# Flamingo block, one core: rows gathered per tile with an inverted slot table, and shared groups split four and three

## Chip, cores and metric

One core of one Trainium2 chip runs the whole program in one launch. The time is device microseconds from the first to the last instruction, with what lies around them; the median of 3 runs stands for the kernel.

## What is computed

Input `x` is 32 sequences of 112 rows of 256 numbers, 3584 rows in all. First comes gated cross attention to a context of 375 rows (16 heads), then a mixture of experts: every row passes through two shared experts and through the two of 14 routed experts that its gate likes best.

```python
x = x + tanh(g_xattn) * xattn(layernorm(x), ctx, Wq, Wk, Wv, Wo, bo)
xf = layernorm(x).reshape(3584, 256)
gates = softmax(xf @ router_w)                 # 14 experts
top_v, top_i = top_k(gates, 2)                 # weights, divided by their sum
routed = sum over the row's two experts of weight * ffn_e(xf)
shared = ffn_s0(xf) + ffn_s1(xf)
x = x + tanh(g_ffn) * (routed + shared)
# ffn(h) = silu((rmsnorm(h) * rms_w) @ W1) @ W2, W1 256x512, W2 512x256
```

## The kernel before

Every product is made of float32r parts: a value is split into a high part (ScalarE's cast) and a low one (VectorE's subtraction), and three matmuls hi*hi, hi*lo, lo*hi are summed.

**Attention** (`attend`, 0 to about 1125 us) goes over 16 pairs of sequences in a loop. SP issues its loads in program order: `x_in` for pair p+2, keys, residual rows, and beside them one routed expert per pair, whose weights POOL scales and splits for `w_split` in HBM. It stores the rows after attention in `x2_rows`, and the normalised rows with one more number in `h_rows` (257 a row). Besides, it prepares the buffer `sorted` in HBM, 69 tiles of 128 rows of 258 numbers: at the start it is filled with zeros from `fill` (L366), and after pair 0 the column D of all its rows is set to the numbers of spare rows, from `spare` (L389), 4 bytes at a time.

**Front** (`front`) transposes all rows, computes the gate, and works on items, one for each group of 512 rows and shared expert: `hidden(i)` is 24 matmuls of 512 columns into four banks, ScalarE's silu and cast, VectorE's subtraction (`split_hidden`), then `output(i)`, 48 matmuls of 256 columns, which VectorE adds to `acc` (`accumulate`). `BEFORE` = 5 groups, 10 items, come here. PE's order is hidden(i), output(i-1). Between its own duties VectorE makes the plan: for each row and choice k the slot (place in the sorted order, in which each expert has whole tiles), and for each of the 69 tiles its expert. When the slots are known, POOL writes to `sorted`: for 14 half groups SP loads the rows to SBUF twice (`load_rows`, 28 loads in four buffers), POOL adds number of destination and weight (L997), and issues 4 indirect DMAs of 128 rows each (L1002), 56 in all.

**Routed stage** (`routed_experts`) goes over 69 tiles. A tile's rows come as one plain load from `sorted`, six buffers ahead, issued by ACT; POOL copies each row's number and weight (`take_meta`); PE transposes the rows, 6 matmuls of 512 columns make the hidden part, 4 transposes, 8 output matmuls; ScalarE and VectorE scale both halves by the weight (L1504, L1538); POOL scatters the 128 result rows to `y_rows` (L1417). Weights of experts stand in a ring of five places; the places also hold the front's buffers, so expert e is loaded only when those are done. `w_ready` is counted in order of the experts.

**Tail** (`shared_after`): the other 2 groups, 4 items. SP loads `y_rows` back (two blocks a group), POOL adds both to `acc` (L1596, 14 additions of 128x1024), VectorE accumulates the shared parts, SP stores the groups.

Of the kernel before, what the change touches and what calls it, by code (L numbers as in the profile page):

```python
# [16 lines left out]
ALU = mybir.AluOpType  # L17
# [34 lines left out]
def fuse_weights(nc, io, sb, banks, ctx):  # L52

    if True:
# [13 lines left out]
        bias_in, bias_ok, fill_ok = sem("bias_in"), sem("bias_ok"), sem("fill_ok")  # L68
        sb["zeroed"], sb["fill_ok"] = zeroed, fill_ok
# [12 lines left out]
        def gpsimd(pool):  # L82
# [5 lines left out]
            nc.gpsimd.memset(sb["fill"][:], 0.0).then_inc(zeroed, 1)  # L88
            nc.gpsimd.iota(sb["spare"][:], pattern=[[P, SLOT_TILES]], base=TOPK * TOK, channel_multiplier=1
                           ).then_inc(fill_ok, 1)  # L90
            pool.wait_ge(zeroed, 2)
            pool.wait_ge(fill_ok, 1)
# [95 lines left out]
def attend(nc, io, sb, banks):  # L188

    with ExitStack() as ctx:  # L190
# [41 lines left out]
        x_landed, slots_filled = sem("x_landed"), sem("slots_filled")  # L232
# [77 lines left out]
        def _(sp):  # L310
# [52 lines left out]
            sp.wait_ge(sb["zeroed"], 2)  # L363
            sp.wait_ge(sb["fill_ok"], 1)
            empty = sb["fill"][:].unsqueeze(1).to_broadcast([P, SLOT_TILES, ROW])
            sp.dma_start(io["sorted"].rearrange("(t p) d -> p t d", p=P), empty).then_inc(slots_filled, 16)  # L366
            load_x(1)

            def body(p, jobs):
# [13 lines left out]
                if not first and not last:  # L383
# [3 lines left out]
            sp.wait_ge(slots_filled, 16)  # L387
# [9 lines left out]
            sp.wait_ge(slots_filled, 32)  # L397
# [302 lines left out]
        def _(dve):  # L700
# [124 lines left out]
            for s in (4, 3, 2, 1):  # L825
# [11 lines left out]
               ("spare", [P, (TOK * TOPK + E * (P - 1)) // P], I32), ("kvT_hi", [P, 2, MW], F32R), ("kvT_lo", [P, 2, MW], F32R),  # L837
# [6 lines left out]
ROW = D + 2  # L844
WSIZE = 2 * HID + 4 * D
RING = 5
BEFORE = 5
COUNT_AFTER = 1
PRODUCTS = [("hi", "hi"), ("lo", "hi"), ("hi", "lo")]
# [28 lines left out]
def front(nc, io, sb, banks, ctx):  # L878

    if True:  # L880
# [21 lines left out]
        meta = buf("meta", [P, TILES, TOPK, 2])  # L902
# [6 lines left out]
        slot_f = buf("slot_f", [P, TILES, TOPK])  # L909
        slot = buf("slot", [P, TILES, TOPK], U32)  # L910
# [5 lines left out]
        acc, rows = sb["acc"], sb["rows"]  # L916

        RB = 4
# [7 lines left out]
        consts, step, counted, meta_ok, slot_ok = sem("consts"), sem("step"), sem("counted"), sem("meta_ok"), sem("slot_ok")  # L926
        acc_landed = [sem(f"acc_landed{i}") for i in range(2)]
        rows_landed = [sem(f"rows_landed{b}") for b in range(RB)]
        rows_sent = [sem(f"rows_sent{b}") for b in range(RB)]
        meta_set = sem("meta_set")  # L930
        h_done, silu_done, hid_hi_ok, hid_lo_ok = sem("h_done"), sem("silu_done"), sem("hid_hi"), sem("hid_lo")
        o_done, acc_done = sem("o_done"), sem("acc_done")
        H_BANK, O_BANK, COUNT_BANK = banks[0:4], banks[4:6], banks[6:8]
# [4 lines left out]
        def sync(sp):  # L938
# [9 lines left out]
            def load_rows(u):  # L948
                two = by_group(io["h_rows"], u // 2)[:, 2 * (u % 2):2 * (u % 2) + 2, 0:D]
                for k in range(TOPK):  # L950
                    sp.dma_start(rows[:, u % RB, :, k, 0:D], two).then_inc(rows_landed[u % RB], 16)

# [8 lines left out]
            for g in range(BEFORE):  # L961
# [4 lines left out]
            for g in range(BEFORE, GROUPS):  # L966
                sp.dma_start(acc[:, 4 * g:4 * g + 4, :], by_group(io["x2_rows"], g)).then_inc(acc_landed[1], 16)
            sp.wait_ge(step, PLAN_END)
            load_experts(sp, io, sb, [0])
            for u in range(RB, 2 * GROUPS):  # L970
                sp.wait_ge(rows_sent[u % RB], 64 * (u // RB))
                load_rows(u)
            for e in (1, 2):
                sp.wait_ge(h_done, 16 * e)
                load_experts(sp, io, sb, [e])

        def gpsimd(pool):
# [11 lines left out]
            for k in range(TOPK):  # L989
                nc.gpsimd.iota(meta[:, :, k, 0].bitcast(I32), pattern=[[4 * P, GROUPS], [1, 4]], base=k * TOK,  # L990
                               channel_multiplier=4).then_inc(meta_ok, 1)
            pool.wait_ge(meta_ok, 2 + TOPK)
            pool.wait_ge(slot_ok, 1)
            for u in range(2 * GROUPS):
                b = u % RB
                pool.wait_ge(rows_landed[b], 32 * (u // RB) + 32)
                nc.gpsimd.tensor_copy(rows[:, b, :, :, D:ROW], meta[:, 2 * u:2 * u + 2, :, :]).then_inc(meta_set, 1)  # L997
                pool.wait_ge(meta_set, u + 1)
                for t in range(2):
                    for k in range(TOPK):  # L1000
                        at = slot[:, 2 * u + t, k:k + 1]
                        nc.gpsimd.indirect_dma_start(io["sorted"], bass.IndirectOffsetOnAxis(ap=at, axis=0),  # L1002
                                                     rows[:, b, t, k, :], None).then_inc(rows_sent[b], 16)

        def tensor(pe):
# [65 lines left out]
            for i in range(len(items)):  # L1071
                hidden(i)
                if i > 0:
                    output(i - 1)
# [37 lines left out]
        def vector(dve):  # L1112
# [667 lines left out]
```

## Time and profile before

| | |
|---|---|
| median of 3 runs (lowest, highest) | 1613.81 us (1612.7, 1614.38) |
| profiled execution | 1619.13 us, its span 1617.4 us |
| mean granted TensorE clock | 0.968 |
| busy in the span | PE 1509.5 us (93%), VectorE 1126.5 (70%), ScalarE 1018.3 (63%), POOL 459.8 (28%) |
| DMA | 160.89 MB, 99 GB/s on average |

A group of instructions is named by line, engine, operation and tile; "idle before" is the time in which its engine waited just before it, with what released it. "issue" means that the profile shows nothing that the engine waited for. The granted clock is a share of full speed, 0.50 being 1.2 GHz and 1.00 being 2.4 GHz. In the table by stretch the columns are PE, weight loads (PEld), VectorE (DVE), ScalarE (ACT) and POOL, then granted clock, busy share of the DMA engines and GB/s.

### The profile page before, as it was taken

What the parts mean: (1) busy time and instruction counts of PE and PEld (TensorE: products, weight loads), DVE (VectorE), ACT (ScalarE), POOL (GpSimd) and SP (SyncE); (2) the same over time, 40 slices, a digit from 0 to 9 for tenths busy, and PEclk for the clock granted to TensorE, in tenths of its full rate; (3) what the DMA queues carried; (4) which work ended last, traced back from release to release, by engine and by line L of the source; (5) the groups of instructions that cost most, each with busy time, mean ns of one, the idle gap of its engine ahead of it and who ended that gap; (6) DMA issues with size and microseconds to landing.
All of it is one profiled execution on the core that took longest, in us unless ns stands there. A gap on an engine that the chain in (4) does not pass through costs nothing. (4 is left out here: it accounts for less than half of the span.)

```text
span 1617.4 us, 34486 instructions
## 1 busy us (share of the span) xinstructions
PE 1509.5 (93%) x10102; PEld 1398.8 (86%) x10102; DVE 1126.5 (70%) x2788; ACT 1018.3 (63%) x2641; POOL 459.8 (28%) x742
## 2 busy tenths in 40 slices
PE   6797999999999999999999999996896689999997
PEld 6697999999999999999999999996684578888887
DVE  5686888788888888888888888884861234444446
ACT  4575777777777777777777777774531235555552
POOL 1003134131241322413314033111047203333338
PEclk9898999999999999999999999998897699999999
DMA  9315302112021121211211202101637435664234
GB/s 266 78 16 40 103 13 97 74 50 97 17 101 66 50 97 39 79 72 44 97 74 44 87 29 97 68 15 52 247 100 215 164 119 180 235 229 134 80 125 192
DMA packets 89921, 160.89 MB, mean 99 GB/s; under 512 B 20688, under 2 KB 73184, under 8 KB 86272
## 3 DMA queue, kind: packets, MB, share of 16 engines
q1 hardware_dynamic: 74784, 135.29, 26.3%
q0 software_dynamic: 6000, 16.45, 2.8%
q10 hardware_dynamic: 9072, 8.33, 1.8%
q8 instruction: 36, 0.59, 0.2%
q14 instruction: 29, 0.24, 0.0%
HBM read 94.06 MB, written 65.98 MB: 99 GB/s over the span
## 5 line engine op out<-in xcount | busy, mean ns | idle before, releaser
L631 ACT ACTIVATE prob<-bank,nmax 112x375 f32<-112x375 f32 x512 | 296.2, 579 | 247.2 <-DVE nmax L720 245.8
L703 DVE TENSOR_TENSOR pT_lo<-bank,pT_hi 125x336 fp32r<-125x336 f32 x512 | 257.0, 502 | 101.8 <-ACT pT_hi L643 99.2
L720 DVE TENSOR_REDUCE nmax<-bank 112x1 f32<-112x375 f32 x512 | 276.4, 540 | 33.7 <-PE bank L499 27.7
L553 PE MATMUL bank<-keep_ident,prob 112*125 112x112 f32 x1536 | 254.4, 274 | 31.1 <-DVE pT_lo L703 30.9
L553 PEld LDWEIGHTS bank<-keep_ident,prob 112*125 112x125 f32 x1536 | 227.0, 189 | 60.3 <-issue 46.2
L643 ACT CAST pT_hi<-bank 125x336 fp32r<-125x336 f32 x512 | 223.4, 436 | 1.3 <-PE bank L553 1.2
L497 PE MATMUL bank<-attend_wvo_hi,zT_hi 128*112 128x256 f32 x512 | 179.2, 350 | 0.6 <-DVE zT_lo L703 0.6
L497 PE MATMUL bank<-attend_kvT_hi,qp_hi 128*112 128x376 f32 x512 | 171.7, 335 | 0.8 <-ACT prob L631 0.7
L498 PE MATMUL bank<-attend_kvT_hi,qp_lo 128*112 128x376 f32 x512 | 171.4, 335 | 0.0
L499 PE MATMUL bank<-attend_kvT_lo,qp_hi 128*112 128x376 f32 x512 | 171.4, 335 | 0.0
L636 ACT ACTIVATE prob<-prob,prob_inv 112x375 f32<-112x375 f32 x256 | 153.4, 599 | 1.6 <-DVE prob_inv L726 0.4
L497 PE MATMUL bank<-xnT_hi,attend_wqk_hi 128*128 128x224 f32 x512 | 141.8, 277 | 3.9 <-DVE xnT_lo L703 3.9
L498 PE MATMUL bank<-attend_wvo_hi,zT_lo 128*112 128x256 f32 x512 | 144.4, 282 | 0.0
L499 PE MATMUL bank<-attend_wvo_lo,zT_hi 128*112 128x256 f32 x512 | 143.8, 281 | 0.0
L497 PE MATMUL bank<-pT_hi,kv_hi 125*128 125x448 f32 x384 | 141.9, 370 | 1.5 <-DVE zT_lo L703 1.5
L499 PE MATMUL bank<-xnT_lo,attend_wqk_hi 128*128 128x224 f32 x512 | 142.7, 279 | 0.0
L498 PE MATMUL bank<-xnT_hi,attend_wqk_lo 128*128 128x224 f32 x512 | 141.8, 277 | 0.0
L499 PE MATMUL bank<-pT_lo,kv_hi 125*128 125x448 f32 x384 | 140.5, 366 | 0.0
L498 PE MATMUL bank<-pT_hi,kv_lo 125*128 125x448 f32 x384 | 140.2, 365 | 0.0
L442 POOL TENSOR_SCALAR rs<-mv 112x1 f32<-112x1 f32 x32 | 7.0, 219 | 439.3 <-DVE mv L774 439.2
L729 DVE TENSOR_SCALAR prob<-prob,prob_inv 112x375 f32<-112x375 f32 x256 | 118.6, 463 | 9.1
L1417 POOL DMA_INDIRECT y_rows<-over_y,keep_tile_meta x69 | 66.7, 967 | 190.7 <-DVE over_y L1538 187.7
(226 smaller groups left out, 3809.1 us busy)
## 6 DMA issues: line engine op xcount, KB each, us to landing
w_split<-we_split SPq DMA_DIRECT2D x14, 2048.0 KB, 6.9
keep_weights<-w_split SPq DMA_DIRECT2D x14, 2048.0 KB
we_in<-in_w SPq DMA_DIRECT2D x28, 512.0 KB, 5.9
sorted<-keep_fill SPq DMA_DIRECT2D x1, 8901.0 KB, 35.3
keep_tile_in<-sorted ACTq DMA_DIRECT2D x63, 129.0 KB
keep_rows<-h_rows SPq DMA_DIRECT2D x28, 256.0 KB
over_y_all<-y_rows SPq DMA_DIRECT2D x14, 512.0 KB, 8.9
kv_in<-in_ctx SPq DMA_DIRECT2D x32, 187.5 KB
```

The lines of the kernel that those rows point to most:

```text
L442: nc.gpsimd.tensor_scalar(rs2[:, 0, 0:1], mv2[:, 1:2], LN_EPS, None, ALU.add).then_inc(ln2_pool, 1)
L497: nc.tensor.matmul(out, a[0], b_[0], start=start, stop=False)
L498: nc.tensor.matmul(out, a[1], b_[0], start=False, stop=False)
L499: return nc.tensor.matmul(out, a[0], b_[1], start=False, stop=stop)
L553: last = nc.tensor.transpose(T[s % 2][0:MP, c * N:(c + 1) * N], prob[:, s % NB, c * MP:(c + 1) * MP], ident[0:N, 0:N])
L631: nc.scalar.activation(prob[:, s % NB, :], S[s % 3][0:N, 0:M], ACT.Exp, bias=nmax[:, s % NB:s % NB + 1], accum_out=psum_[:, s % NB:s % NB ...
L636: nc.scalar.mul(prob[:, s % NB, :], prob[:, s % NB, :], pinv[:, s % NB:s % NB + 1]).then_inc(norm_act, 1)
L643: nc.scalar.copy(dst, T[s % 2][0:MP, 0:MC * N].rearrange("p (c n) -> p c n", c=MC)).then_inc(pT_hi, 1)
L703: return nc.vector.tensor_tensor(dst, src, hi.bitcast(F32), ALU.subtract)
L720: nc.vector.tensor_reduce(nmax[:, s % NB:s % NB + 1], S[s % 3][0:N, 0:M], AX, ALU.max, negate=True).then_inc(max_ready, 1)
L729: nc.vector.tensor_scalar(prob[:, s % NB, :], prob[:, s % NB, :], pinv[:, s % NB:s % NB + 1], None, ALU.mult).then_inc(norm_dve, 1)
L1417: nc.gpsimd.indirect_dma_start(io["y_rows"], bass.IndirectOffsetOnAxis(ap=at, axis=0), y[:, t % YB, :], None).then_inc(y_sent[t % YB], 16)
```

## The change

`sorted`, its fill, the spare numbers, the 28 loads and the 56 scatters are gone. Instead the plan is inverted on the chip: for each of the 7168 pairs of row and choice the slot is divided into tile number and lane (place in the tile). 56 columns of 128 pairs are taken in 14 chunks of 4. For a chunk VectorE (`make_hot`) compares with counting numbers, which gives a one-hot matrix of lanes (128x128 a column) and one of tiles, the latter times two numbers that name the row; PE multiplies them (`place_rows`, 4 matmuls of 138 columns a chunk) and sums all in one bank. `decode` makes `from_row` and `to_row` of it, for each of the 69 tiles 128 numbers. POOL then gathers a tile's rows from `h_rows` with an indirect DMA (`fetch`), six ahead, and then one behind every scatter. The weights are no longer applied in the tile but in the tail, where VectorE adds `y_all` times weight (56 operations of 128x256) in POOL's place. Four shared groups are ahead of the routed tiles (8 items) and three behind them (6 items). The buffers lie elsewhere: expert 1's place is free after h_done 16 as before, expert 2's when decode is done.

```diff
@@ attend: sync @@
-            sp.wait_ge(sb["zeroed"], 2)
-            sp.wait_ge(sb["fill_ok"], 1)
-            empty = sb["fill"][:].unsqueeze(1).to_broadcast([P, SLOT_TILES, ROW])
-            sp.dma_start(io["sorted"].rearrange("(t p) d -> p t d", p=P), empty).then_inc(slots_filled, 16)
             load_x(1)
...
-            spare_rows = io["sorted"].rearrange("(t p) d -> p t d", p=P)[:, :, D:D + 1]
-            sp.dma_start(spare_rows, sb["spare"][:].bitcast(F32).unsqueeze(2), allow_slow_non_contiguous=True
-                         ).then_inc(slots_filled, 16)
@@ sizes @@
-BEFORE = 5
+BEFORE = 4
+COLS = TOPK * TILES
+CHUNK = 4
+CHUNKS = COLS // CHUNK
+CHUNKS_IN = {3: (0, 1, 2), 4: (3, 4, 5, 6), 5: (7, 8, 9, 10), 6: (11, 12, 13)}
@@ front: sync @@
-            sp.wait_ge(w_lo, 6)
-            for u in range(RB):
-                load_rows(u)
...
             sp.wait_ge(step, PLAN_END)
+            sp.wait_ge(nums_ok, 4)
+            sp.wait_ge(lanes, 4)
             load_experts(sp, io, sb, [0])
-            for u in range(RB, 2 * GROUPS):
-                sp.wait_ge(rows_sent[u % RB], 64 * (u // RB))
-                load_rows(u)
-            for e in (1, 2):
-                sp.wait_ge(h_done, 16 * e)
-                load_experts(sp, io, sb, [e])
+            sp.wait_ge(h_done, 16)
+            load_experts(sp, io, sb, [1])
+            sp.wait_ge(rows_of_ok, 2)
+            load_experts(sp, io, sb, [2])
@@ front: tensor @@
+            def place_rows(c):
+                pe.wait_ge(hot_ok, 3 * c + 3)
+                for m in range(CHUNK):
+                    last = nc.tensor.matmul(PLACE_BANK[:, 0:2 * SLOT_TILES], lane_hot[:, c % 2, m, :],
+                                            tile_hot[:, c % 2, m, :, :].rearrange("p n t -> p (n t)"),
...
+                last.then_inc(hot_used, 1)
             for i in range(len(items)):
                 hidden(i)
+                for c in CHUNKS_IN.get(i - 1, ()):
+                    place_rows(c)
                 if i > 0:
                     output(i - 1)
...
+            output(len(items) - 1)
             sb["turn_first_rows"](pe)
-            output(len(items) - 1)
@@ front: vector @@
+            def make_hot(c):
...
+                if c >= 2:
+                    dve.wait_ge(hot_used, c - 1)
...
+                nc.vector.tensor_tensor(placed[:], up_to(SLOT_TILES), each(tile_no, SLOT_TILES), ALU.is_equal).then_inc(tile_eq, 1)
+                nc.vector.tensor_tensor(lane_hot[:, b, :, :], up_to(P), each(lane_no, P), ALU.is_equal).then_inc(hot_ok, 1)
+                dve.wait_ge(tile_eq, c + 1)
+                for n in range(2):
+                    nc.vector.tensor_tensor(tile_hot[:, b, :, n, :], placed[:], each(place[n], SLOT_TILES), ALU.mult
+                                            ).then_inc(hot_ok, 1)
             plan_owner()
+            for c in CHUNKS_IN[3]:
+                make_hot(c)
             for i in range(4, len(items)):
                 for j in range(4):
                     split_hidden(i, j)
+                if i - 1 == max(CHUNKS_IN):
+                    decode()
                 for t in range(4):
                     accumulate(i - 1, t)
+                for c in CHUNKS_IN.get(i, ()):
+                    make_hot(c)
@@ routed_experts: gpsimd @@
+            def fetch(t):
+                if t >= HB:
+                    pool.wait_ge(h_turned, t - HB + 1)
+                at = sb["from_row"][:, t:t + 1]
+                nc.gpsimd.indirect_dma_start(h_in[:, t % HB, :], None, io["h_rows"], bass.IndirectOffsetOnAxis(ap=at, axis=0)
+                                             ).then_inc(h_landed[t % HB], 16)
+            pool.wait_ge(sb["sem_rows_of_ok"], 2)
+            for t in range(HB):
+                fetch(t)
@@ shared_after @@
+        Y_IN = {1: order[0:2], 2: order[2:4], 3: order[4:6], 4: order[6:7]}
-                    nc.gpsimd.tensor_tensor(whole, whole, y_all[:, k, 4 * g:4 * g + 4, :], ALU.add).then_inc(y_added, 1)
+            def add_routed(g):
+                dve.wait_ge(y_landed[g], 32)
+                for k in range(TOPK):
+                    for t in range(4 * g, 4 * g + 4):
...
+                        nc.vector.scalar_tensor_tensor(out=acc[:, t, :], in0=y_all[:, k, t, :],
+                                                       scalar=sb["weight_of"][:, k, t:t + 1], in1=acc[:, t, :],
+                                                       op0=ALU.mult, op1=ALU.add).then_inc(y_added, 1)
```

VectorE in the front, after the plan: before (a row is a run of like instructions; L1302 is `split_hidden`, L1297 `accumulate`):

```order
L1270 CAST keep_ring_of<-over_owner 1x69
L1302 TENSOR_TENSOR keep_hid_lo<-keep_silu,over_hid_hi 128x512 x4
L1297 TENSOR_TENSOR keep_acc<-bank,keep_acc 128x256 x4
L1302 TENSOR_TENSOR keep_hid_lo<-keep_silu,over_hid_hi 128x512 x4
L1297 TENSOR_TENSOR keep_acc<-bank,keep_acc 128x256 x4
```

and now, where each chunk is four rows and the first three chunks stand ahead of item 4's splits (L1340):

```order
L1308 CAST keep_ring_of<-over_owner 1x69
L1257 TENSOR_TENSOR over_placed<-over_count_up,over_tile_no 128x276
L1258 TENSOR_TENSOR over_lane_hot<-over_count_up,over_lane_no 128x512
L1261 TENSOR_TENSOR over_tile_hot<-over_placed,over_place_4920 128x4x69
L1261 TENSOR_TENSOR over_tile_hot<-over_placed,over_place_4921 128x4x69
...
L1340 TENSOR_TENSOR keep_hid_lo<-keep_silu,over_hid_hi 128x512 x4
L1335 TENSOR_TENSOR keep_acc<-bank,keep_acc 128x256 x4
L1257 TENSOR_TENSOR over_placed<-over_count_up,over_tile_no 128x276
```

The run of splits that came right behind the plan now comes behind three chunks, and between the splits of items 4, 5, 6 and 7 stand four, four and three chunks.

POOL, from the front into the routed stage, before:

```order
L997 COPY keep_rows<-front_meta 128x4x2
L1002 DMA sorted<-keep_rows,front_slot 8832x258 x4
L1408 COPY keep_tile_meta<-keep_tile_in 128x2 x3
L1417 DMA y_rows<-over_y,keep_tile_meta 16000x256
L1408 COPY keep_tile_meta<-keep_tile_in 128x2
```

and now:

```order
L979 CAST over_pad_row<-over_pad_i 128x69
L1446 DMA keep_tile_in<-h_rows,keep_from_row 128x257 x6
L1455 DMA y_rows<-over_y,keep_to_row 16000x256
L1446 DMA keep_tile_in<-h_rows,keep_from_row 128x257
L1455 DMA y_rows<-over_y,keep_to_row 16000x256
```

The copies went, and a gather follows each scatter; the 56 scatters in the front have nothing in their place.

VectorE in the tail now (before, L1639 and L1646 stood there alone; L1676 is `add_routed`):

```order
L1685 TENSOR_TENSOR keep_hid_lo<-keep_silu,over_hid_hi 128x512 x8
L1676 SCALAR_TENSOR_TENSOR keep_acc<-over_y_all,keep_weight_of,keep_acc 128x256 x16
L1668 TENSOR_TENSOR keep_acc<-bank,keep_acc 128x256 x4
L1685 TENSOR_TENSOR keep_hid_lo<-keep_silu,over_hid_hi 128x512 x4
L1676 SCALAR_TENSOR_TENSOR keep_acc<-over_y_all,keep_weight_of,keep_acc 128x256 x16
```

Two groups' additions stand behind the splits of items 1, 2 and 3 each, and one group's behind those of item 4.

## Rows read from the trace of the kernel before

**Rows 1.** Page, part 2: PE busy, in tenths, in 40 slices of 40.4 us
```profile
PE   6797999999999999999999999996896689999997
```

**Rows 2.** Busy time by stretch: start:end, length; then each engine's us (x instructions)
```profile
50.00:60.00 10.00, 5.43 (x23) 5.44 (x24) 5.13 (x16) 4.10 (x13) 0.26 (x2) 0.50 0.12 42
1153.00:1211.00 58.00, 54.39 (x313) 47.86 (x314) 43.96 (x99) 26.50 (x43) 14.72 (x18) 0.94 0.46 157
1211.00:1273.00 62.00, 31.85 (x111) 22.25 (x111) 5.89 (x12) 4.99 (x9) 43.82 (x53) 0.66 0.68 219
1250.00:1270.00 20.00, 5.22 (x12) 3.16 (x11) 0.00 (x0) 0.00 (x0) 14.64 (x18) 0.50 0.65 232
1273.00:1323.00 50.00, 47.10 (x306) 43.71 (x305) 18.79 (x37) 19.45 (x33) 0.98 (x3) 0.94 0.32 110
1357.00:1557.00 200.00, 200.00 (x1174) 172.38 (x1173) 93.75 (x176) 107.36 (x236) 68.21 (x118) 1.00 0.47 161
1563.00:1609.00 46.00, 45.07 (x292) 41.04 (x291) 33.91 (x31) 20.02 (x33) 38.05 (x16) 1.00 0.55 214
```

**Rows 3.** DMA issues, 0 to 100 us, and PE's timeline, 50 to 56 us
```profile
sorted<-keep_fill SPq DMA_DIRECT2D x1, 8901.0 KB, 35.3
...
54.57 0.94 PE L553 MATMUL bank<-keep_ident,prob 112*125 112x112 f32 x3 [9.48 <-DVE pT_lo L703]
```

**Rows 4.** Timeline of SP's queue (start, length of issue), and a DMA issue
```profile
101.94 0.43 SPq L315 DMA_DIRECT2D x_in<-in_x  x1
...
178.74 0.35 SPq L315 DMA_DIRECT2D x_in<-in_x  x1
...
245.15 0.35 SPq L315 DMA_DIRECT2D x_in<-in_x  x1
...
sorted<-attend_spare SPq DMA_DIRECT2D x1, 34.5 KB, 16.8
```

**Rows 5.** Chain of waits in the front (start, us, what), and a DMA queue, 1211 to 1273
```profile
1156.61 14.27 PE bank L865 x48
...
1189.04 5.60 PE bank L865 x24
...
1314.42 5.69 PE bank L873 x48
...
1323.50 2.94 PE bank L1437 x6
...
q8 instruction: 1, 0.02, 0.1%
```

**Rows 6.** Groups of instructions, 1120 to 1617 us: busy us, mean ns, idle before
```profile
L1002 POOL DMA_INDIRECT sorted<-keep_rows,front_slot x56 | 55.0, 983 | 16.7 <-issue 14.2 <-POOL keep_rows L997 2.5
...
L1596 POOL TENSOR_TENSOR keep_acc<-keep_acc,over_y_all 128x1024 f32<-128x1024 f32 x14 | 37.6, 2703 | 7.0 <-DMA over_y_all<-y_rows 6.4
...
L1538 DVE SCALAR_TENSOR_TENSOR over_y<-bank,keep_tile_meta,over_y 128x256 f32<-128x256 f32 x69 | 33.4, 484 | 33.8 <-ACT over_y L1504 33.8
...
L1646 DVE TENSOR_TENSOR keep_hid_lo<-keep_silu,over_hid_hi 128x512 fp32r<-128x512 f32 x16 | 28.7, 1822 | 7.4 <-ACT over_hid_hi L1627 7.4
L1302 DVE TENSOR_TENSOR keep_hid_lo<-keep_silu,over_hid_hi 128x512 fp32r<-128x512 f32 x40 | 27.5, 690 | 31.2 <-ACT over_hid_hi L1110 22.3 <-issue 8.9
...
L1297 DVE TENSOR_TENSOR keep_acc<-bank,keep_acc 128x256 f32<-128x256 f32 x40 | 15.1, 418 | 61.0 <-remote 49.1 <-PE bank L873 11.8
...
L1161 DVE TENSOR_TENSOR over_tie<-over_gate_prob,front_top 128x392 f32<-128x392 f32 x2 | 1.1, 568 | 0.1
```

**Rows 7.** Tile `keep_tile_meta`, 1340 to 1567 us: the scatters' time to landing
```profile
DMA to landing us min/median/max: 2.4/2.4/3.1
```

**Rows 8.** Chain of waits from 1560 us (one row), and PE's timeline in the tail
```profile
1560.06 0.44 PE bank L1445 x4
...
1563.48 0.39 PE L865 MATMUL bank<-keep_hT_hi,keep_w1s_hi 128*128 128x512 f32 x1
...
1603.43 0.39 PE L873 MATMUL bank<-keep_w2s_hi,over_hid_hi 128*128 128x256 f32 x1 [0.93 <-DVE keep_hid_lo L1646]
```

More of the change, by code:

```diff
@@ L908, in front @@
         offset = buf("offset", [P, E])
-        slot_f = buf("slot_f", [P, TILES, TOPK])
-        slot = buf("slot", [P, TILES, TOPK], U32)
+        slot_f, slot_i = sb["slot_f"], sb["slot_i"]
+        tile_no, lane_no = sb["tile_no"], sb["lane_no"]
+        count_up_i, count_up = sb["count_up_i"], sb["count_up"]
+        place_i, place = [sb["place_i0"], sb["place_i1"]], [sb["place0"], sb["place1"]]
+        pad_i, pad_row = sb["pad_i"], sb["pad_row"]
+        block_f, from_f, to_f = sb["block_f"], sb["from_f"], sb["to_f"]
+        lane_hot, tile_hot, placed = sb["lane_hot"], sb["tile_hot"], sb["placed"]
         tile_i = sb["tile_i"]
@@ L915, in front @@
         hs, hid = sb["silu"], {q: sb["hid_" + q] for q in ("hi", "lo")}
-        acc, rows = sb["acc"], sb["rows"]
-        RB = 4
+        acc = sb["acc"]
         h_landed = [sem(f"h_landed{g}") for g in range(GROUPS)]
@@ L988, in gpsimd @@
             nc.gpsimd.iota(tile_i[:], pattern=[[1, SLOT_TILES]], base=0, channel_multiplier=0).then_inc(consts, 1)
[L989 to L1003, printed above, removed]
+            nc.gpsimd.iota(count_up_i[:], pattern=[[1, P]], base=0, channel_multiplier=0).then_inc(nums_i, 1)
+            nc.gpsimd.iota(place_i[0][:].rearrange("p (g t) -> p g t", t=4), pattern=[[0, TOPK * GROUPS], [1, 4]], base=0,
+                           channel_multiplier=4).then_inc(nums_i, 1)
+            nc.gpsimd.iota(place_i[1][:].rearrange("p (g t) -> p g t", t=4), pattern=[[1, TOPK * GROUPS], [0, 4]], base=1,
+                           channel_multiplier=0).then_inc(nums_i, 1)
+            nc.gpsimd.iota(pad_i[:], pattern=[[P, SLOT_TILES]], base=TOPK * TOK, channel_multiplier=1).then_inc(nums_i, 1)
+            pool.wait_ge(nums_i, 4)
+            for made, whole in ((count_up, count_up_i), (place[0], place_i[0]), (place[1], place_i[1]), (pad_row, pad_i)):
+                nc.gpsimd.tensor_copy(made[:], whole[:]).then_inc(nums_ok, 1)
+            pool.wait_ge(nums_ok, 4)
         def tensor(pe):
@@ L1379, in routed_experts @@
         HT_BANK, H_BANK, T_BANK, O_BANK = banks[0:2], banks[2:4], banks[4:6], banks[6:8]
-        rows = io["sorted"].rearrange("(t p) d -> p t d", p=P)
-        def load_rows(eng, t):
-            eng.dma_start(h_in[:, t % HB, :], rows[:, t, :]).then_inc(h_landed[t % HB], 16)
         def sync(sp):
-            for b in range(4):
-                sp.wait_ge(sb[f"sem_rows_sent{b}"], 64 * len(range(b, 2 * GROUPS, 4)))
-            for t in range(HB):
-                load_rows(sp, t)
             sp.wait_ge(sb["sem_h_done"], 8 * BEFORE)
@@ L1589, in gpsimd @@
         def gpsimd(pool):
[L1590 to L1596 removed]
+            pool.wait_ge(y_added, 4 * TOPK * GROUPS)
         def tensor(pe):
@@ L1647, in vector @@
                                             hid["hi"][:, e, j, :].bitcast(F32), ALU.subtract).then_inc(hid_lo_ok, 1)
-            for i in (len(items) - 2, len(items) - 1):
-                accumulate(i)
+                if i + 1 == len(items):
+                    accumulate(i - 1)
+                for n in Y_IN.get(i, ()):
+                    add_routed(n)
+            accumulate(len(items) - 1)
             dve.wait_ge(acc_done, 4 * len(items))
@@ L1717, in scratch @@
 def scratch(nc, io):
-    for name, shape in (("x2_rows", (TOK, D)), ("h_rows", (TOK, HW_ROW)), ("sorted", (SLOT_TILES * P, ROW)),
+    for name, shape in (("x2_rows", (TOK, D)), ("h_rows", (TOK, HW_ROW)),
                         ("w_split", (E, P, 2 * WSIZE)), ("y_rows", (TOPK * TOK + SLOT_TILES * P, D))):
@@ L1740, in build @@
                 sb["acc_at"] = nc.sbuf_base - 4 * TILES * D
-            if n == "rows":
-                sb["rows_at"] = nc.sbuf_base - 4 * 8 * TOPK * ROW
+            if n == "stage":
+                sb["stage_at"] = nc.sbuf_base - 4 * STAGE
+            if n == "hid_lo":
+                sb["hid_lo_at"] = nc.sbuf_base - 4 * 8 * HID
             if n == "weights":
```

161 lines of the change are left out of this document (90 added, 71 removed).

## The prediction

> **What bounds the kernel now.** Read first the page's view of 40 slices [rows 1]: PE is at nine tenths or more nearly everywhere, and thin in four places: the first 60 us, slice 4 (around 150 us), slice 28 (from the attention stage to the front, which the change does not touch) and slices 31 and 32 (1213 to 1294 us). Slices 29 and 33 also fall short, at either end of the front. Then the table by stage [rows 2]: routed stage 200.00 of 200 us busy at granted clock 1.00, tail 45.07 of 46, but between 1211 and 1273 us only 31.85 of 62 at clock 0.66. So PE's own work bounds all but those places, and the change is judged by what it does to PE's idle time there and to PE's work.
>
> **Attention start.** The fill of `sorted` (8901 KB) lands 35.3 us after it is issued; `x_in` of pair 1 stands behind it on the same queue. PE's gap of 9.48 us at 54.57 ends with DVE, which had waited for that `x_in` [rows 3]. After it the clock is 0.50 for 50 to 60 us [rows 2]: 5.43 us of matmuls at half speed, 2.7 us lost. The change removes fill and `spare` write; the other loads are the same. I take 9.5 + 2.7 = 12.2 us back; at least the gap alone, 9.5.
>
> **Pair 1.** The `spare` write, elements of 4 bytes each, takes 16.8 us to land. `x_in` is issued once a pair: 76.80 us apart across that write, 66.41 at the next pair [rows 4]. Take 10.4 back; pairs with no such write vary by about 1 us, so no less than 9. The attention stage gives **22.6 us**.
>
> **Front.** Chain of waits [rows 5]: an item (24 hidden, 48 output matmuls) is 5.60 + 5.69 = 11.29 us; the first 48 hidden matmuls take 14.27, 3.1 above two times 5.60; from 1156.61 to the first routed matmul at 1323.50 are 166.9 us; from the last output (1314.42 + 5.69 = 1320.1) to it 3.4. So 166.9 - 112.9 (ten items) - 3.1 - 3.4 = 47.5 us, of which some 1.3 are the counting; **46 us** are gaps that the profile calls "issue": PE waits for nothing shown. They lie where the 28 loads of `rows` and the 56 scatters run together: between 1211 and 1273 POOL ran 53 instructions, about 43 of them scatters (four follow each copy). From 1273, when they are over, PE is busy 47.10 of 50 us [rows 2]. The change has none of these loads, and no indirect transfer until the table is decoded near the end of item 7. I take all 46 back; the lower bound is nothing, for the trace names no cause.
> Two items move behind the routed stage: -22.6 us here.
> Added here: 14 chunks. DVE: `lane_hot` (128x512) like the split of the same size, 690 ns; the three 128x276 operations between 1/2 of that and the 568 ns of 128x392 [rows 6], say 450. That is 2.04, with waits 2.1 us a chunk. PE: 56 matmuls of 138 columns, between the transposes' 0.44 us for four and the 5.69 us for 48 of 256 columns [rows 5, 8]: 0.11 to 0.12 each, 6.4 us. There are two buffers. PE multiplies the chunks of item i only after `hidden(i+1)`, so DVE can make two ahead, and makes the others while PE waits: one chunk (3 made) at items 4 and 7, two (4 made) at 5 and 6. Idle: 6 x 2.1 = 12.6, less some 0.6 that overlaps: 12. Adding 6.4 gives **+18.4 us**. The least is 6.4 (DVE makes them in its idle time); the most is 14 x 2.1 + 6.4 = 36. DVE's splits behind `make_hot` come late too, but PE has 5.69 us of outputs in front of it before it needs them.
> At the end `output(7)` now stands ahead of the first row transposes. Decode follows the last splits (about 6 us after `hidden(7)`): ten small DVE operations, for which no row stands and 0.3 us each are allowed. The first gather then needs POOL's 0.98 [rows 6] and, like a scatter, 2.4 us to land [rows 7]: near 12.4 us. PE reaches the transposes at 2.6 + 2 x 5.69 = 14. Nothing, or +0.6 for the transposes and the cast after `output(7)`. Cover for this is the two outputs; a late gather would show whole.
> Front: -46 - 22.6 + 18.4 + 0.6 = **-49.6 us**.
>
> **Routed stage.** Each of 69 tiles costs POOL a scatter and now a gather: 2 x (0.98 + 0.30) = 2.6 us (983 ns, and 14.2 us of gaps over 47, [rows 6]) in a tile of 3.41 us (200 us with 1174 matmuls, 20 a tile; [rows 2]). The metadata copy, ACT's DMA issue and its wait go. Six buffers give a gather two tiles. Bytes stay as they are. PE's work is unchanged and PE is never idle here, so 0. Nothing excludes a small gain or loss; I allow 3 us either way.
>
> **Tail.** PE's part starts at 1563.48, four items with one idle of 0.93 [rows 8], so it ends at 1609.5, 7.9 us ahead of the end of the span. POOL's 14 additions of 2703 ns run beside it (37.6 us) and stretch DVE's splits from 690 to 1822 ns [rows 6]. They now become 56 operations on DVE of at most 484 ns: 27.1 us, plus six items of 4 x 0.69 + 4 x 0.42 (418 ns) = 4.4 us: 54 us beside 67.7 us of PE. Hidden by PE. So 6 x 11.29 in place of 46.1: **+21.7 us**; the last store follows the last accumulate as before.
>
> **Sum:** -22.6 - 49.6 + 0 + 21.7 = -50.5. The profiled execution, 1619.13 us (span 1617.4), becomes 1568.6; it stands 5.3 above the median of the runs, 1613.81, which becomes **1563**.
>
> **A rule on the clock.** In the front PE would stand idle four times, 2 to 4 us each. Before, the granted clock fell to 0.66 over a stretch with PE half idle, and stayed at 0.94 where it was busy 54.39 of 58 us [rows 2]. I keep full clock: with 12 us idle in 60, these stops lie nearer the second row. The Trainium skill, TensorE: Matmul & The Clock Gate, "What's actually happening", says that idleness brings the array back to 1.2 GHz. By that rule each stop would be followed by a slow start like the front's first, 3.1 us, and the result would be 1575.
>
> **Rivals.**
> (a) The clock falls at the stops, or DVE's chunks cost more than 2.1 us: 4 x 3.1 = 12, 1575. For: PE stops for chunks by construction.
> (b) The 46 us do not go, because the gaps come from something that stays, such as the 2048 KB loads of experts. For: they are worst from 1250 to 1270 us, where PE does 12 matmuls in 20 us [rows 2], and the last row loads are over by then. Against: in the routed stage, where the other experts are loaded, PE is busy 200.00 of 200 us. 1563 + 46 = 1609. 
> (c) **Slower:** the gaps come from indirect transfers issued closely. The routed stage now issues 138 instead of 69. Price: 46 us for 43 scatters, 1.07 us each; 69 gathers make +74, result 1637. It decides from 50.5 / 69 = 0.73 us a gather. For: the gaps stop with the last scatter. Against: the first scatters, before 1211, came just as closely (983 ns and 0.3 apart), and PE was busy 54.39 of 58 us [rows 2]; in the routed stage there will be one per 1.7.
> (d) The tail turns DVE-bound: a group pair of additions (7.7 us) with its item's 4.4 exceeds PE's 11.29 by 0.8 in three items, and the first waits for `y_all`. Up to 8 us: 1571.
>
> **How the numbers follow.** Forecast 0.50; (a) 0.17; (d) 0.08; (b) 0.12, partly or whole; (c) 0.10, more if partial; no change at all 0.03. The range takes in the least cost of the chunks (-12, with a little from the routed stage: 1547) and (b) at the top: 1547 to 1609. Outside are (c) and the extremes. Faster 0.88, same 0.03, slower 0.09; within 0.2% (3 us) a measurement of this kernel cannot tell from no change.
>
> **What would show it.** Right: `x_in` issues 66 us apart from pair 0 on, no PE gap near 50 us; in the front no "issue" gaps, but four waits for `tile_hot`, 2 us at items 4 and 7 and 4 us at 5 and 6; 69 tiles in about 236 us; six items in the tail in 68 us with DVE's splits at 690 ns. Wrong: "issue" gaps on PE beside gathers; PE waiting for `tile_in`; granted clock at 0.5 in the front; DVE at nine tenths in the tail.

## Result, and the profile after

The changed kernel takes **1577.83 us** (median of 4 runs, 1575.0 to 1579.01) where the kernel before takes 1614.1 (4 runs, 1612.7 to 1618.27): ratio **0.9769, 95% interval 0.9746 to 0.9791**. Forecast were 1563, with a range of 1547 to 1609. The profiled execution took 1576.96 us, its span 1574.9, against 1619.13 and 1617.4 before.

The page of the changed kernel, part 2: PE and its clock in 40 slices, now of 39.4 us (before: [rows 1]):

```profile
PE   6999999999999999999999999997798799999999
...
PEclk9999999999999999999999999999898999999999
```

Slice 4 is no longer thin. Slices 31 and 32, both at 6 before, show 8 and 7; 28 and 29, where the attention stage gives over to the front, stay thin. The stretches, as in [rows 2] (start:end, length, then each engine's us, the clock, the DMA share and GB/s):

```profile
50.00:60.00 10.00, 9.77 (x72) 9.23 (x71) 8.53 (x23) 7.99 (x22) 2.42 (x5) 1.00 0.02 2
1180.00:1251.00 71.00, 57.48 (x371) 53.13 (x369) 40.35 (x95) 17.04 (x29) 5.94 (x6) 0.91 0.28 115
1251.00:1410.00 159.00, 149.27 (x835) 124.16 (x836) 63.50 (x124) 74.25 (x168) 78.38 (x80) 0.99 0.57 201
1410.00:1504.00 94.00, 93.92 (x541) 79.99 (x540) 41.76 (x81) 45.97 (x107) 49.04 (x51) 1.00 0.25 72
1504.00:1571.00 67.00, 67.00 (x437) 61.09 (x435) 46.25 (x103) 29.35 (x49) 1.87 (x2) 1.00 0.42 162
```

The third row is what the forecast did not have: in the first two thirds of the routed stage PE is idle 9.7 us of 159, of which 7.3 are waits for gathers and the rest lies at the stage's start. Before, it was never idle from 34 us into the stage on [rows 2]. In the last third it is busy again.

The chain of waits of the changed kernel gives the stages' borders (compare [rows 5, 8]):

```profile
1132.41 12.82 PE bank L853 x48
...
1251.36 2.94 PE bank L1477 x6
...
1504.53 10.92 PE bank L853 x48
```

In PE's timeline the first matmul of the tail starts at 1504.37. With the borders of before (1156.61, 1323.50, 1563.48, end 1617.4):

| stage | before | after | difference | forecast |
|---|---|---|---|---|
| to the first hidden matmul | 1156.6 | 1132.4 | -24.2 | -22.6 |
| front, to the first routed matmul | 166.9 | 119.0 | -47.9 | -49.6 |
| routed stage | 240.0 | 253.0 | +13.0 | 0 |
| tail, to the end | 53.9 | 70.5 | +16.6 | +21.7 |
| sum | 1617.4 | 1574.9 | -42.5 | -50.5 |

**The routed stage.** The chain shows the same five rows again and again; here is one turn of it:

```profile
1277.85 0.99 POOL y_rows L1455
1279.14 6.36 DMA keep_tile_in<-h_rows,keep_from_row
1285.55 0.44 PE bank L1464 x2
...
1292.45 0.99 POOL y_rows L1455
1293.75 6.30 DMA keep_tile_in<-h_rows,keep_from_row
```

The scatter of tile t is issued, 1.3 us later the gather of tile t + 6, and PE's transposes (L1464) start only when that has landed, 6.3 us on. They would have been due at 1284.88, one tile (3.47 us) after those of 1281.41: the gather has 5.7 us and needs 6.4. There are nine such turns, from 1279 to 1402, landing in 6.2 to 7.3 us. SP's queue in the same stretch has nine loads of experts (start of the first, time to the last):

```profile
1276.79 122.90 SPq L1400 DMA_DIRECT2D keep_weights<-w_split  x9
```

Nine loads between 1276.8 and 1399.7, nine late gathers. This is a correlation; the run with small loads of experts tests it.

**The front.** No gap called issue between matmuls of an item is left. PE's waits in the front and groups of the vector engine there (busy us, mean ns, idle before):

```profile
PE bank L1051 <- DVE over_tile_hot L1261: 8.0, 6, 1.4
PE bank L853 <- DVE keep_w2s_lo L1324: 4.0, 1, 4.0
PE bank L1477 <- issue: 3.5, 1, 3.5
PE bank L1464 <- DMA keep_tile_in<-h_rows,keep_from_row: 2.3, 1, 2.3
```
```profile
L1261 DVE TENSOR_TENSOR over_tile_hot<-over_placed,over_place 128x276 fp32r<-128x276 f32 x28 | 11.1, 439 | 0.0
L1258 DVE TENSOR_TENSOR over_lane_hot<-over_count_up,over_lane_no 128x512 fp32r<-128x512 f32 x14 | 9.6, 684 | 0.0
L1257 DVE TENSOR_TENSOR over_placed<-over_count_up,over_tile_no 128x276 f32<-128x276 f32 x14 | 6.2, 443 | 5.9 <-PE bank L1051 5.4
```

Six waits for `tile_hot`: one at items 4 and 7, two at items 5 and 6, as the two buffers demand. The chain at items 5 and 6 and the clock behind the stop:

```profile
1190.34 5.52 PE bank L853 x24
1195.86 0.42 PE bank L1051 x4
...
1199.98 0.67 PE bank L1051 x4
1200.65 7.21 PE bank L861 x48
...
1239.27 8.10 DMA keep_tile_in<-h_rows,keep_from_row
```
```profile
1195.00:1201.00 6.00, 3.39 (x23) 2.96 (x22) 4.60 (x10) 0.38 (x1) 0.00 (x0) 0.97 0.01 3
1201.00:1208.00 7.00, 7.00 (x49) 6.96 (x48) 2.37 (x6) 1.95 (x4) 0.00 (x0) 0.78 0.00 0
```

The 48 output matmuls behind a stop take 7.21 us instead of 5.67, with the granted clock at 0.78 while PE is busy all the time. The last row of the chain is the first gather: 8.1 us from issue to landing. It does not run alone: the same end of the decode that releases it also frees expert 2's place, and SP's queue issues two loads of experts 0.9 us ahead of it. From 1239 to 1247 the DMA engines are 98% busy:

```profile
1238.33 0.81 SPq L1400 DMA_DIRECT2D keep_weights<-w_split  x2
...
1239.00:1247.00 8.00, 6.08 (x52) 5.87 (x51) 0.76 (x2) 0.00 (x0) 5.94 (x6) 1.00 0.98 369
```

**The tail.** The vector engine's groups, to be read beside [rows 6, 8]:

```profile
L1676 DVE SCALAR_TENSOR_TENSOR keep_acc<-over_y_all,keep_weight_of,keep_acc 128x256 f32<-128x256 f32 x56 | 22.5, 478 | 0.0
L1685 DVE TENSOR_TENSOR keep_hid_lo<-keep_silu,over_hid_hi 128x512 fp32r<-128x512 f32 x24 | 16.3, 690 | 12.9 <-ACT over_hid_hi L1656 12.9
```

The splits are back at 690 ns (1822 beside POOL's additions), and PE has no idle time in the tail.

### The profile page after: what moved, and what is told of

Read it like the earlier page. It is cut to its first block and busy times, and to the rows that moved or that the text cites. A ratio compares the mean times of both kernels' runs of the same rounds, so it can differ in the third digit from the quotient of the medians.

```text
span 1574.9 us, 34494 instructions
## 1 busy us (share of the span) xinstructions
PE 1503.3 (95%) x10158; PEld 1395.2 (89%) x10158; DVE 1147.8 (73%) x2912; ACT 1011.1 (64%) x2641; POOL 419.8 (27%) x662
## 5 line engine op out<-in xcount | busy, mean ns | idle before, releaser
L1561 DVE TENSOR_TENSOR over_tile_hT_lo<-bank,over_tile_hT_hi 128x256 fp32r<-128x256 f32 x69 | 29.3, 425 | 124.9 <-ACT over_tile_hT_hi L1522 73.1
```

## Experiments

They came in three sets, each on one chip, with runs of the kernel before on the same chip. What that kernel took is part of the finding: 1582 us in the first set (one run), 1609 to 1616 (median 1612.7 of seven) in the second, 1619 to 1625 in the third.

### First set: one transfer or one stage at a time

**Fill and spare write put back into the changed kernel.**

```diff
             load_res(0, 1)
+            empty = sb["fill"][:].unsqueeze(1).to_broadcast([P, SLOT_TILES, D + 2])
+            sp.dma_start(io["sorted"].rearrange("(t p) d -> p t d", p=P), empty).then_inc(slots_filled, 16)
             load_x(1)
...
             body(0, FULL)
+            sp.dma_start(spare_rows, sb["spare"][:].bitcast(F32).unsqueeze(2), allow_slow_non_contiguous=True
+                         ).then_inc(slots_filled, 16)
```

> The changed kernel with the fill and the spare write of before put back in their places on SP's queue; nothing reads what they write. Theory: these two transfers alone are the gain of the attention stage. Then x_in is issued 76 to 77 us apart across the spare write (66.0 without it), PE stands idle 9 to 10 us near 54 us, and the front's first hidden matmul starts 22 to 25 us later than the 1132.41 us of the changed kernel, near 1156; the time is about 1601. Rival: part of the 24.2 us has another source (the order of allocation, the other loads, drift between executions); then the start moves by clearly less, 15 or below.

Measured: 1599.4 us (one run). First hidden matmul at 1154.68, 22.3 us later than the 1132.41 of the first trace, which was not taken beside it. The one trace without the fill from this set's chip (the run with small loads, below) starts at 1136.48, 18.2 earlier. PE's idle time near 54 us is back, and so is the long crossing in SP's queue (x_in):

```profile
53.87 0.94 PE L553 MATMUL bank<-keep_ident,prob 112*125 112x112 f32 x3 [9.27 <-DVE pT_lo L703]
...
101.57 0.43 SPq L315 DMA_DIRECT2D x_in<-in_x  x1
...
176.72 0.35 SPq L315 DMA_DIRECT2D x_in<-in_x  x1
...
243.16 0.35 SPq L315 DMA_DIRECT2D x_in<-in_x  x1
```

75.2 us across the spare write and 66.4 at the next pair. The two transfers make most of the stage's gain, some 18 us. The rival (the start moves by 15 us or less) falls by either comparison, but what it named as drift between executions is there too and accounts for the rest of the 24.2.

**The loads of experts cut to 16 KB** (changed kernel, routed stage).

```diff
-                load_experts(sp, io, sb, [e])
+                sp.dma_start(sb["weights"][:, e % RING, 0:32].bitcast(F32), io["w_split"][e][:, 0:32]
+                             ).then_inc(sb["w_landed"][e % RING], 16)
```

> The changed kernel with the loads of experts 5 to 13 in the routed stage cut from 2048 KB to 16 KB (the weights are stale from then on; the work and its order are the same). Theory A: a gather takes 6 to 7 us to land because the 2048 KB loads share the DMA engines with it. Then none of the nine waits of PE for tile_in is left, and the stage is 7 to 10 us shorter, 243 to 246 us in place of 253.2. Theory B: a gather is slow by itself, or behind the scatter in its queue; then waits of 6 to 7 us on gathers stay and the stage stays above 250. The remaining 3.8 us (3.47 in place of 3.41 us a tile) stay under both unless they too come from the loads.

Measured: 1571.17 us; the routed stage from 1254.54 to 1498.62 is 244.1 us, and PE's waits in it are these:

```profile
PE bank L1478 <- issue: 3.5, 1, 3.5
PE bank L1478 <- DVE over_tile_hT_lo L1562: 1.4, 2, 1.1
```

None is for `tile_in`, while the run with the fill, on the same chip and with full loads, waits nine times for gathers, 8.4 us in all, and has 252.4 us in the stage. Theory A holds in this: a gather is late only with a 2048 KB load in flight. Whether the two meet in the DMA engines or in the memory behind them was not tried. The steady tile stays at 3.473 us, so the smaller part of the loss has another source.

**Row loads without refills, and no scatters** (kernel before). What are the 46 us of gaps in its front? The first kernel leaves out the ten later refills of the row buffers, so that its scatters send stale rows. The second leaves out the scatters; its row loads wait for POOL's copy alone, and all its tiles are padding.

```diff
-            for u in range(RB, 2 * GROUPS):
-                sp.wait_ge(rows_sent[u % RB], 64 * (u // RB))
-                load_rows(u)
...
-                pool.wait_ge(rows_landed[b], 32 * (u // RB) + 32)
+                if u < RB:
+                    pool.wait_ge(rows_landed[b], 32)
+                else:
+                    pool.wait_ge(rows_sent[b], 64 * (u // RB))
```

> The kernel before with the row loads of the front made only for its first four buffers; the ten later refills are left out, and the 56 scatters send what is in the buffers (so the rows sorted are partly the wrong ones). It asks what made the 46 us of issue gaps on PE. If it is the scatters: the gaps stay, 40 us or more, and the time is within 6 us of before. If it is the row loads, or loads and scatters in flight together: the gaps fall below 15 us, and the time is 30 to 45 us shorter, near 1575 to 1590.

```diff
-                for t in range(2):
-                    for k in range(TOPK):
-                        at = slot[:, 2 * u + t, k:k + 1]
-                        nc.gpsimd.indirect_dma_start(io["sorted"], bass.IndirectOffsetOnAxis(ap=at, axis=0),
-                                                     rows[:, b, t, k, :], None).then_inc(rows_sent[b], 16)
...
-                sp.wait_ge(rows_sent[u % RB], 64 * (u // RB))
+                sp.wait_ge(meta_set, u - RB + 1)
```

> The kernel before without the 56 scatters of the front (all row loads stay and now wait for the copy of the metadata alone; every slot is then a padding slot, and the last stage reads the spare rows). If the scatters make the issue gaps: the gaps go, the front is some 46 us shorter, near 1570. If the row loads make them: they stay at 20 us or more, though the loads now follow one another faster and the gaps may lie in a shorter stretch. If both are needed together: the gaps go here and in the run without refills too.

Measured: 1578.8 and 1568.89 us (one run each), and in neither a gap. But the run of before beside them took only 1582.29, so both could be read as showing nothing: on this chip the gaps seemed not to exist. The theory "loads and scatters together" was the reading of the moment; it did not survive the third set.

### Second set: the trace of before again, and two repairs

**The kernel before, unchanged.**

> The kernel before, unchanged, for its trace beside the first four experiments, whose runs of it took 1582 us where 1613.81 us had been measured. Theory: the 46 us of issue gaps on PE in the front are not a fixed part of this kernel; here they are mostly absent. Then the front takes 125 to 135 us from the first hidden matmul to the first routed one instead of 166.9, with the last scatter (about 1270) rather than PE as what releases the first routed tile, and attention, routed stage and tail are as in the first trace. Rival: the missing 32 us lie elsewhere (attention or routed stage), and the front still shows 40 us of gaps.

The expectation that the gaps would be absent failed: this set landed on another chip, and they were back. 1605.98 us, the front 1152.32 to 1308.73, 156.4 us, PE's waits called issue 16.5 + 5.3 us.

**The changed kernel, unchanged.**

> The changed kernel, unchanged, timed in rounds against before. Where before shows no issue gaps, of the measured gain of 36 us what the gaps made must be missing: 24 us from the attention stage and nothing else large, less the tail's 16.5 and the routed stage's 13; I expect 1575 to 1579 for the changed kernel and a ratio of 0.994 to 0.999 if before stays at 1582, 0.977 if before is back at 1614.

1579.08 us (4 runs, 1575.37 to 1580.92), ratio 0.979 (0.9764 to 0.9816), near the 1575 to 1579 and the 0.977 expected for a chip with gaps.

**Gathers issued earlier.**

```diff
-            for t in range(HB):
+            for t in range(HB + 2):
                 fetch(t)
             for t in range(SLOT_TILES):
+                if t + HB + 2 < SLOT_TILES:
+                    fetch(t + HB + 2)
                 pool.wait_ge(y_ready, t + 1)
...
-                if t + HB < SLOT_TILES:
-                    fetch(t + HB)
```

> The changed kernel with each gather issued up to three tiles earlier: POOL issues the gather of tile t + 8 ahead of the scatter of tile t, as soon as its buffer is free, in place of the gather of tile t + 6 behind it. Theory: the gather has 5.7 us from issue to use and needs 6 to 7 when a load of an expert is in flight; with some 15 us it is never late. Then PE has no wait for tile_in from the second tile on, the routed stage takes 243 to 246 us in place of 253, and the time falls by 7 to 10 us. Rival: the gathers only queue up on the same engines and are late all the same, or the earlier issue takes bandwidth from the loads of the experts, and PE waits for weights: less than 3 us gained.

1573.2 us (1570.88 to 1573.57) against 1579.08 on the same chip, 5.9 less, where 7 to 10 were expected. The routed stage is 245.6 us (1252.89 to 1498.50) where the unchanged one has 252.6 (1253.00 to 1505.59): 7.0 less, inside the 243 to 246 that were expected. In the stage no wait for `tile_in` is left; the one before it, for the first gather, is (2.2 us).

**With it, the chunks of the front spread.**

```diff
-CHUNKS_IN = {3: (0, 1, 2), 4: (3, 4, 5, 6), 5: (7, 8, 9, 10), 6: (11, 12, 13)}
+CHUNKS_IN = {3: (0, 1, 2, 3), 4: (4, 5, 6, 7), 5: (8, 9, 10, 11), 6: (12, 13)}
...
-                for c in CHUNKS_IN.get(i - 1, ()):
+                for c in CHUNKS_IN.get(i - 1, ())[:2]:
                     place_rows(c)
                 if i > 0:
                     output(i - 1)
+                for c in CHUNKS_IN.get(i - 1, ())[2:]:
+                    place_rows(c)
```

The vector engine makes the second two behind the splits of the next item.

> As the run with early gathers, and the 14 chunks of the front are spread: per item two are multiplied behind the hidden matmuls as now and two behind the output matmuls, so that the vector engine makes those while PE does outputs (4, 4, 4, 2 chunks in items 3 to 6, in place of 3, 4, 4, 3). Theory: PE's stops for chunks (2.9, 4.8, 5.1 and some 3 us) and the half clock behind them (1.6 us each) come from PE having nothing in between. Then the front is 12 to 18 us shorter than in the changed kernel (about 119 us), and the time is near 1555 to 1558 together with the early gathers. Rival: DVE itself is the bound (4 chunks of 2.2 us, 4 splits, 4 adds are 13 us an item against 13.1 of PE), so that waits move to the splits; gain of 5 us or less.

**1559.41 us** (4 runs, 1556.35 to 1560.06), ratio to before 0.9666 (0.9643 to 0.9689): 19.7 us less than the changed kernel beside it and 13.8 less than with early gathers alone, though just above the expected 1555 to 1558. The front is 104.6 us (1137.58 to 1242.20) against 119.7, 15.1 less; 2.3 of these are the wait for the first gather, which is gone too. Its chain:

```profile
1200.81 5.67 PE bank L861 x48
1206.48 0.85 PE bank L1051 x8
1207.33 5.54 PE bank L853 x24
1212.87 0.85 PE bank L1051 x8
1213.72 5.67 PE bank L861 x48
```
```profile
1180.00:1242.00 62.00, 57.73 (x401) 53.30 (x400) 45.29 (x112) 19.70 (x33) 6.90 (x7) 1.00 0.37 144
```

Every chunk pair costs PE its 0.85 us and nothing more, the outputs are at 5.67 again and the clock is 1.00. Only at the first chunks, where the plan's last operations stand ahead of them, the splits come late.

### Third set: the cause of the gaps, on one chip

> The kernel before again, for a trace on the same chip as the next two. The runs without refills and without scatters had no issue gaps, but shared a chip on which the run of before took 1582 us; its unchanged trace on another chip had them (1604 us of span). So the comparison needs all three on one chip. Expected: on a chip where this run is above 1600 us, 20 to 35 us of gaps called issue on PE between 1200 and 1275 us; where it is near 1582, under 8 us of them.

> As the first run without refills, on the chip of the unchanged kernel above. If the scatters alone make the gaps where a chip shows them: 30 us or more of gaps, over 1600 us. If loads and scatters in flight together make them: under 5 us of gaps, and 1577 to 1582 us, as on the first chip, whatever the unchanged kernel takes.

> As the first run without scatters, on the chip of the unchanged kernel above. If the row loads make the gaps where a chip shows them: 20 us or more of them, over 1585 us. If both are needed: under 5 us of gaps and 1567 to 1572 us, as on the first chip.

> The changed kernel beside them. It has no row loads and scatters in its front, so it should take 1575 to 1580 us on any chip; the ratio to before is then set by the gaps of before alone: 0.977 to 0.98 where before takes 1609 to 1614 us, 0.995 to 0.999 where it takes 1582.

One run each but for the last:

| kernel | time | front | PE busy, 1211 to 1266 or 1273 |
|---|---|---|---|
| before | 1618.84 | 173.7 | 24.38 of 62 |
| no refills | 1623.72 | 175.9 | 16.14 of 55 |
| no scatters | 1569.54 | 120.5 | 61.59 of 62 |
| changed | 1584.09 (2 runs; ratio 0.9765, 0.9711 to 0.9819) | 119.9 | |

The kernel without refills, on this chip and then on that of the first set: the same code, the same stretch.

```profile
1211.00:1266.00 55.00, 16.14 (x33) 9.06 (x33) 1.73 (x4) 1.22 (x2) 39.51 (x48) 0.51 0.31 108
```
```profile
1211.00:1266.00 55.00, 54.37 (x352) 49.26 (x350) 21.25 (x40) 23.83 (x40) 43.36 (x50) 1.00 0.46 160
```

Third set, chain of waits: the scatters, 1.28 us apart, are nearly all that the DMA engines carry, and PE gets a matmul through every 2 to 4 us. The last scatter is issued at 1260.92, and soon after it lands PE is at speed:

```profile
1252.37 2.43 issue
1254.80 0.37 PE bank L873
1255.17 2.42 issue
...
1260.78 3.82 issue
1264.60 0.37 PE bank L873
...
1267.40 6.34 PE bank L873 x31
```

So the scatters make the gaps and the row loads do not: the expectation "loads and scatters together" is refuted, and the changed kernel's expected 1575 to 1580 us on any chip was missed too (1584.09). Where the gaps appear they need only the scatters; on the first chip 56 scatters in 76.6 us (73.1 here) left PE's matmuls alone, and only the first routed tile waited 6.3 us for its rows. The fetching of instructions, which rival (b) named, does not show in the gaps: from 1211 to 1266 the instruction queues moved one packet in the run with gaps (third set) and five in the same kernel without them (first set). The changed kernel's front does not depend on the chip: with its chunks in their first order it takes 118.1 to 119.9 us in all six traces, though its routed stage was 256.7 us on this chip (waits for gathers 7.9 us, 5.0 in the second set). What differs from one chip, or one loading of the program, to the next is open, and it was not tried whether wider spacing would end the gaps.

## Why the prediction was right and where it was wrong

The sign, the mechanism of each stage but one and the range were right. The time is 14.8 us above the forecast: on the profiled executions' account 8.0 of it (-42.5 instead of -50.5); the rest lies in the step from profiled execution to median. That took 5.3 off; the changed kernel's profiled execution is 0.9 below its own median. The gaps of before vary (fronts of 156.4, 166.9 and 173.7 us in three traces), and the change takes away exactly that part. Where they are nearly absent its gain should be too: on the first set's chip the kernel before took 1582.29 and the changed kernel with the fill 1599.4, so that without the fill's 18.2 to 22.3 an estimate is 1577 to 1581, a gain of 1 to 5 us; the changed kernel itself was not run there. That the forecast gain was met at all rests on the luck of a chip, or a loading, with gaps.

**Attention: right in kind, its size met by luck.** -24.2 against -22.6, but the two first traces lie at the far ends of what executions show: over eight traces with the fill the front's first hidden matmul starts between 1149.5 and 1156.6, over six without it between 1132.4 and 1137.6. The means are 18.7 apart, and within each set, on one chip, 16 to 18. Both terms were too large. The first (12.2 said) is 10.2: so much earlier is the third `x_in` issued on average. The second (10.4 said) is 7.6: with the spare write the next one comes 75.0 us later on average, without it 67.3. The trace that the prediction read had the longest of the eight crossings, 76.80.

**Front: right in sum, by errors that cancel.** The 46 us of gaps went whole, and rival (b) is out: the 2048 KB loads have stayed and nothing of the gaps has. The prediction read them as time in which PE waits. Only 30.0 us of it are that, in PE's waits of the kernel before from 1156.6 to 1323.5:

```profile
PE bank L873 <- issue: 19.1, 18, 2.4
PE bank L865 <- issue: 10.9, 15, 1.8
```

The other 16 are matmuls at a lower clock: PE is busy 133.3 us in that front and 117.1 in the front without scatters of the third set, with the same matmuls (mean granted clock 0.84 and 0.97). The 14 chunks were put at 18.4 us; the four stops took 2.9, 4.8, 5.1 and 2.8 us, 15.6 with the placing matmuls in them; of the 12 us of idle time that were said, 8.0 came. The vector engine's 2.1 us a chunk was 684 + 3 x 440 ns = 2.0 busy, and less than that on the path, since each operation starts before the one ahead has ended. The clock was put at nothing; it cost 1.6, 1.5 and 1.3 us behind the first three stops, 4.4 in all, and nothing behind the last. That is rival (a), by a third of its 12: it came true in kind. Which stop pays is not fixed: over the six traces with these stops the loss is 3.5 to 5.8 us in all, the first stop costs nothing in four of them, the last costs 1.5 in one, and the dearest single one costs 2.6, not 3.1. The Trainium skill (TensorE: Matmul & The Clock Gate, "What's actually happening") says that idleness takes the array back to 1.2 GHz; the traces agree in part, for the same 1.4 us of idle time was followed by a lower clock in some (0.76) and by 1.00 in others. With chunks spread the clock row shows 1.00. The front's first 48 hidden matmuls took 12.82 us where 14.27 were carried over. The change of stage cost 6.4 us between the end of the outputs and the first routed matmul instead of 4.0. The decode was cheaper than allowed (1.5 us from 1236.82, not 3), and the step that failed is the landing: "like a scatter, 2.4 us to land" was 8.1, beside the loads that the same decode releases, so PE waited 2.3.

**Routed stage: wrong, +13.0 where 0 was said.** Two steps failed. First, "six buffers give a gather two tiles", checked against nothing: two tiles less the scatter's 1.3 us are 5.7, and the landing was taken over from the scatters [rows 7], which need 2.4. Gathers need 6.2 to 7.3 while an expert is loaded. This was listed among the signs of error ("PE waiting for `tile_in`"), but had no price and no rival. It is worth 7.0 us by the run with early gathers; the run with small loads has 244.1 us in the stage, 8.3 less than the run with the fill on the same chip. Second, the tile itself: 3.4145 us in every trace of before and 3.473 in every trace of the changed kernel, without late gathers and without large loads too, 0.058 x 69 = 4.0 us. With the 7.3 us of waits that is 11.3 of the 13.0; part of the rest is that a tile behind a late gather is longer by more than the wait (1281.41 to 1285.55 is 4.14 us, 0.67 over 3.47, for a wait of 0.50). PE is not idle in the steady tile; its operations are a little longer (six hidden matmuls 1.40 instead of 1.37). The cause is open; nothing here tells the place of the tiles in memory from the second indirect transfer.

**Rival (c) is out for the gathers, and its premise holds in part.** The gaps do come from indirect transfers issued closely, on chips that show them. But two of them in 3.47 us, 138 in the stage, gave no such gaps in any of the seven traces of the changed kernel and its variants (waits called issue of at most 0.3 us, three at most in a steady stage), among them one from the chip that had the worst gaps in the front of before. What separates 1.28 us apart from 1.7 on average, or a scatter into `sorted` from the others, was not tried.

**Tail: right in kind, 5.1 too dear.** PE's six items took 66.7 us (67.7 said), and the end comes 3.8 us behind PE, not 7.9. "The last store follows the last accumulate as before" was the faulty step: before, the chain's end was POOL's additions, and these are gone. Rival (d) is out: the vector engine is busy 46.25 of 67 us.

## What to carry to other kernels

A transfer that is fetched just in time is to be priced against the worst traffic beside it, not by the landing of its neighbour in a quiet stretch; where its buffer is free earlier, issue it earlier, ahead of the instruction that waits (here 7 us for an exchange of two lines). Work that two engines do by turns is split, so that each has its own work in between: the same 14 chunks, spread, made the front 15.1 us shorter, and the clock stays up. Before a gap that no wait explains goes into a sum, take the trace on more than one chip: the front of before was 36 to 53 us longer than without scatters in three traces, and by a run of 1582 us this can be nearly absent; a gain that rests on it rests on the chip. The same holds for a price read from one trace: the crossing of 76.80 us was the longest of eight, 1.9 above their mean.

## What was not expected of the hardware

- Scatters 1.28 us apart slowed PE to 16.14 us of work in 55 at clock 0.51 on one chip, and left it 54.37 of 55 at clock 1.00 on another: 1623.72 and 1578.8 us for the same kernel. The profile calls the gaps issue and names no resource.
- A gather of 128 rows took 6.2 to 7.3 us to land beside a 2048 KB load and 8.1 as the first of six, with two such loads issued 0.9 us before it, where the kernel before's scatters had needed 2.4 [rows 7].
- After a stop for chunks, in which PE was idle for 1.4 to 2.6 us, the next 48 output matmuls took 7.0 to 7.2 us instead of 5.67 at a granted clock of 0.76 to 0.81, though PE was never idle in them. After the last stop (1.4 us idle, like the first) the clock stayed at 1.00 and they ran at full speed. In other traces of the same front this falls otherwise: 8.23 us at 0.67 behind the second stop and 5.67 behind the first in the second set.
